# Third layer's probabilities turned by VectorE and DMA, the context one step later, and the context's split moved in the second feed-forward

## The chip, the cores and the metric

The kernel runs on one core of a Trainium2 chip. The metric is the time of one execution in device microseconds. Three runs of the kernel before gave 2253.87, 2254.23 and 2256.28 us; their median is 2254.23 us.

## What is computed

Four transformer layers run one after the other on x (16 batches of 128 tokens, 256 wide) and a context of the same shape. The change touches the third layer (called l2 in the code) and the feed-forward of the second (l1). The third layer has two cross-attentions in a row, with 16 heads of width 128, over 16 batches (cut from the reference):

```
qh = (q_in @ wq + bq)   kh = (kv_in @ wk + bk)   vh = (kv_in @ wv + bv)
kh, vh = each with one more key/value row (bias_k, bias_v)
logits = einsum('bqhk,bthk->bhqt', qh, kh) / sqrt(128)
weights = softmax(logits)
ctx = einsum('bhqt,bthk->bqhk', weights, vh);  x = x + ctx @ wo + bo
```

The kernel computes this per head and per group of four batches: 2 attentions x 16 heads x 4 groups = 128 steps. The einsum with vh sums over the 128 keys, so TensorE needs the probabilities with the keys on the partitions, while softmax leaves them with the queries on the partitions. Somewhere between the two they have to be turned.

## The kernel before

`attention2` is one block in which every engine runs its own part of one written list, `order2()`. The loop variable p is the place in the list and `step(stage, behind)` puts the stage of step s = p - behind there. Each engine executes in this order only the stages that it has a function for, so the list is the program of all five engines. What follows are the names that matter here.

At place p TensorE (PE) multiplies the queries (`query`, bank q_psum), then half of the output projection of an older step (`out_a`, o_psum), the keys (`key`, k_psum), the other half (`out_b`), then `turn` (L766: four 128x128 transposes of probs into t_psum, one instruction per batch), `score` (L756), half of a value projection (`value_a`), `context` (L776, probabilities times values into c_psum) and `value_b`. Products in full precision are three matmuls of high and low parts (L114 and L790). `turn` belongs to step p-1, `context` to p-1, and `out_a`/`out_b` to p-2.

VectorE (DVE) at place p makes the low part of the context (L910), the share of each probability (L933, L935), adds the value bias (`values_kept`, L920), adds the two output halves to x (L929), copies t_psum into PT (L901) and takes the maximum of the scores (L905). ScalarE (ACT) makes Q, K, the exponents into the one buffer probs (L833) and the high part of the context (L828). GpSimd (POOL) splits the weights of the heads ahead of their use (L664, L667). SyncE (SP) only issues DMAs: heads, value weights and value rows.

After 128 steps the pipeline drains over a few more places, and a block ends when all five engines have arrived.

The feed-forward of the second layer is the block before. Its list, `FEED_ORDER`, has four groups of eight `up` products and four `down` products. At its end GpSimd runs `split_context` (L2861, L2864): it splits the raw context, 2 x 2048 columns per partition, into the high and low parts that the third layer's keys and values need.

Of the kernel before, what the change touches and what calls it, by code (L numbers as in the profile page):

```python
# [426 lines left out]
STEPS2 = 2 * H * 4  # L427
HEAD_SLOTS = 6
# [13 lines left out]
def order2():  # L442
# [10 lines left out]
    def values(i):  # L453
        return [("value_a", 0, i), ("value_b", 0, i), ("values_kept", 0, i)]

    steps = [("stats", 0), ("value_weights", 0), ("scaled", 0), ("heads", 0), *values(0), ("stats", 1),
             ("normed", 0, 0), *values(1), ("normed", 0, 1), ("key", 0), ("heads", 1), *values(2), ("query", 0),
             ("biased", 0), ("heads", 2), ("heads", 3)]
    for p in range(STEPS2 + 6):
# [17 lines left out]
        step("out_b", 2)  # L477
        step("turn", 1)
# [5 lines left out]
        step("context", 1)  # L484
# [9 lines left out]
def attention2(c):  # L494
# [12 lines left out]
    with ExitStack() as ctx:  # L507
# [29 lines left out]
        PT = sb("PT", [P, BANK])  # L537
# [28 lines left out]
        t_full, t_free = sem("t_full"), sem("t_free")  # L566
        c_full, c_high, c_free = sem("c_full"), sem("c_high"), sem("c_free")
# [36 lines left out]
        def _(sync):  # L604
# [22 lines left out]
            def heads(j):  # L627
# [4 lines left out]
            def value_weights(n):  # L632
# [3 lines left out]
                if 2 <= n + 1 < 8:  # L636
                    sync.wait_ge(v_free, value_at["value_b", 4 * (n - 1) + 3, 3] + 1)
                    load_rows(n + 1)

            order.run({"heads": heads, "value_weights": value_weights})  # L640
# [69 lines left out]
        def _(pe):  # L710
# [58 lines left out]
            def values_summed(s):  # L769
                u, hh = s // 4, s % 4  # L770
                pe.wait_ge(t_free, turn_at["turn", s] + 1)
# [3 lines left out]
                for i in range(4):  # L775
                    last = pe.matmul(c_bank[:, i * S:(i + 1) * S], V[:, u % 2, i, hh * P:(hh + 1) * P],  # L776
                                     PT[:, i * S:(i + 1) * S], start=True, stop=True)
                last.then_inc(c_full, 1)

            def out(s, half):  # L780
# [3 lines left out]
                if n:  # L784
                    pe.wait_ge(o_free, n)
                for i in out_halves(s, half):
                    for m, (left, right) in enumerate(((0, 0), (0, 1), (1, 0))):
                        if left:
                            pe.wait_ge(c_free, s + 1)
                        last = pe.matmul(o_bank[:, i % 2 * D:(i % 2 + 1) * D], context[left][:, i * S:(i + 1) * S],  # L790
                                         wo[right], start=(m == 0), stop=(m == 2))
# [16 lines left out]
        def _(act):  # L808
# [28 lines left out]
            def probs_a(s):  # L837
                act.wait_ge(max_done, s + 1)
                if s:
                    act.wait_ge(t_full, turn_at["turn", s - 1] + 1)  # L840
# [32 lines left out]
        def _(dve):  # L873
# [23 lines left out]
            def turn(s):  # L897
                dve.wait_ge(t_full, turn_at["turn", s] + 1)
                if s:
                    dve.wait_ge(c_full, s)  # L900
# [2128 lines left out]
```

## Time and profile before

| | us |
|---|---|
| median of three runs | 2254.23 |
| the profiled execution, its own time | 2256.25 |
| its span (first to last instruction) | 2254.1 |
| the third layer's attention, from first SP issue to the block's end | 700.2 to 1739.4 |
| TensorE busy over the span | 2136.9 (95%) |
| VectorE busy | 1452.7 (64%) |
| ScalarE busy | 1279.3 (57%) |
| GpSimd busy | 651.8 (29%) |

The profile is one execution, so the sum of a prediction is made against 2256.25 us, and the median lies 2.0 us lower. TensorE's matmuls are pipelined: each row shows a duration that contains latency, and neighbouring rows overlap. What one costs the pace of a full TensorE is the distance between starts, not the duration.

### The profile page before, as it was taken

Reading aid. Unit: us, or ns where it says so; the run is one execution under the profiler, and the core shown is the slowest. Engines: PE = TensorE matmul, PEld = TensorE weight load, DVE = VectorE, ACT = ScalarE, POOL = GpSimd, SP = SyncE. Lnnn points to the kernel's source line nnn. Section 1 sums busy time; section 2 is a strip of 40 time slices with the busy share of each in tenths; the row PEclk is TensorE's granted clock in tenths of the full one; section 3 lists DMA queues with packets and bytes.
Section 4 is the critical chain, followed back from the end, with each engine's and each line's share of the span. In section 5 each row is a group of like instructions: output and inputs, shape, how many; then the busy total and the mean of one; then the engine's idle time right before and its main releaser. Section 6 shows DMA issues by size and latency. Waiting matters only on the chain. (4 is left out here: it accounts for less than half of the span.)

```text
span 2254.1 us, 47742 instructions
## 1 busy us (share of the span) xinstructions
PE 2136.9 (95%) x18208; PEld 1784.1 (79%) x18208; DVE 1452.7 (64%) x2828; ACT 1279.3 (57%) x3300; POOL 651.8 (29%) x661
## 2 busy tenths in 40 slices
PE   6999979999896999999999999999998999999899
PEld 4666656888685888888888888888887886776688
DVE  5788844555444756666666766666666449999963
ACT  3777754566543554444445544444455448988853
POOL 4444321111116422020303312030101127677711
PEclk9999999999998999999999999999998999999999
DMA  4000010000102000010100000000002120000000
GB/s 131 21 16 11 2 54 5 2 2 2 39 1 80 24 24 24 10 38 1 48 1 24 24 24 24 10 29 1 1 1 74 39 58 1 2 2 2 2 10 29
DMA packets 33661, 50.58 MB, mean 22 GB/s; under 512 B 2592, under 2 KB 22048, under 8 KB 32416
## 3 DMA queue, kind: packets, MB, share of 16 engines
q1 hardware_dynamic: 33440, 47.53, 6.9%
q8 instruction: 151, 2.47, 0.5%
q14 instruction: 70, 0.57, 0.1%
HBM read 45.43 MB, written 2.10 MB: 21 GB/s over the span
## 5 line engine op out<-in xcount | busy, mean ns | idle before, releaser
L833 ACT ACTIVATE l_probs<-l_s_psum,l_neg_max 128x129 f32<-128x129 f32 x512 | 183.1, 365 | 267.4 <-DVE l_neg_max L905 267.4
L929 DVE TENSOR_TENSOR x<-x,l_o_psum 128x512 f32<-128x512 f32 x256 | 174.9, 683 | 182.3 <-PE l_o_psum L790 182.3
L910 DVE SCALAR_TENSOR_TENSOR l_context_low<-l_c_psum,cols,l_context_high 128x512 fp32r<-128x512 f32 x128 | 95.8, 749 | 177.4 <-ACT l_context_high L828 177.2
L1461 DVE TENSOR_REDUCE l_neg_max<-l_psum 128x2 f32<-128x512 f32 x256 | 163.5, 683 | 50.2 <-PE l_psum L1251 49.8
L664 POOL TENSOR_TENSOR l_head_w_high<-l_head_raw,one 128x768 fp32r<-128x768 f32 x30 | 44.5, 1483 | 502.6 <-PE l_o_psum L790 502.6
L2513 POOL TENSOR_TENSOR l_probs<-l_probs,l_mask_add 128x512 f32<-128x512 f32 x128 | 161.7, 1284 | 76.9 <-DVE l_probs L2741 76.9
L821 ACT ACTIVATE l_KT<-l_k_psum,cols 128x512 f32<-128x512 f32 x128 | 88.1, 688 | 167.4 <-PE l_k_psum L114 167.4
L1390 ACT ACTIVATE l_PT<-l_psum 128x512 f32<-128x512 f32 x256 | 132.2, 602 | 56.9 <-PE l_psum L1279 56.9
L2683 ACT ACTIVATE l_probs<-l_probs,l_neg_max 128x128 f32<-128x128 f32 x512 | 159.7, 395 | 5.5 <-DVE l_neg_max L2748 5.1
L790 PE MATMUL l_o_psum<-l_head_w_high,l_context_high 128*128 128x256 f32 x512 | 144.7, 283 | 2.5 <-DVE x L929 1.7
L790 PE MATMUL l_o_psum<-l_head_w_high,l_context_low 128*128 128x256 f32 x512 | 144.2, 282 | 2.0 <-DVE l_context_low L910 2.0
L776 PEld LDWEIGHTS l_c_psum<-l_PT,values 128*128 128x128 f32 x1024 | 134.7, 192 | 12.5 <-DVE l_PT L901 1.9
L790 PE MATMUL l_o_psum<-l_head_w_low,l_context_high 128*128 128x256 f32 x512 | 143.5, 280 | 0.0
L114 PE MATMUL l_v_psum<-l_value_w_high,ctx_high 128*128 128x512 f32 x256 | 123.0, 480 | 15.2 <-DVE l_value_w_low L950 14.8
L776 PE MATMUL l_c_psum<-l_PT,values 128*128 128x128 f32 x1024 | 136.1, 276 | 0.9 <-DVE l_PT L901 0.8
L756 PE MATMUL l_s_psum<-l_KT,l_QT 128*128 128x129 f32 x1024 | 135.6, 274 | 0.8 <-ACT l_QT L815 0.8
L815 ACT ACTIVATE l_QT<-l_q_psum,l_query_bias 128x512 f32<-128x512 f32 x128 | 88.5, 691 | 76.0 <-PE l_q_psum L114 76.0
L756 PEld LDWEIGHTS l_s_psum<-l_KT,l_QT 128*128 128x128 f32 x1024 | 124.5, 191 | 1.2 <-ACT l_QT L815 1.2
L2132 DVE TENSOR_TENSOR l_mlp_h_low<-l_mlp_h,l_mlp_h_high 128x512 fp32r<-128x512 f32 x96 | 71.5, 747 | 72.6 <-ACT l_mlp_h L2046 71.9
L114 PE MATMUL l_mlp_psum<-l_mlp_w_high,l_mlp_h_high 128*128 128x256 f32 x384 | 111.0, 289 | 6.5 <-DVE l_mlp_h_low L2132 6.5
L2043 ACT ACTIVATE l_mlp_h_high<-l_mlp_psum,cols 128x512 fp32r<-128x512 f32 x96 | 66.2, 690 | 88.0 <-PE l_mlp_psum L114 80.5
L114 PE MATMUL l_mlp_psum<-l_mlp_w_high,l_mlp_h_low 128*128 128x256 f32 x384 | 109.6, 286 | 0.0
(320 smaller groups left out, 6343.0 us busy)
## 6 DMA issues: line engine op xcount, KB each, us to landing
l_head_raw<-in_l_heads SPq DMA_DIRECT2D x32, 384.0 KB, 3.0
l_w<-in_l_w SPq DMA_DIRECT2D x4, 1024.0 KB, 9.6
l_ctx_in<-in_ctx_T SPq DMA_DIRECT2D x16, 256.0 KB, 5.5
l_value_raw<-in_l_values SPq DMA_DIRECT2D x8, 512.0 KB, 3.7
l_value_rows<-in_l_rows SPq DMA_DIRECT2D x8, 512.0 KB, 4.9
l_x_in<-in_x_T SPq DMA_DIRECT2D x16, 128.0 KB, 2.2
l_x_in<-in_ctx_T SPq DMA_DIRECT2D x16, 128.0 KB, 2.7
values<-in_l_w SPq DMA_DIRECT2D x2, 1024.0 KB, 6.2
```

What stands on the lines that cost most here:

```text
L114: last = pe.matmul(out, left[a], right[b], start=(start and n == 0), stop=(stop and n == 2))
L756: last = pe.matmul(scores[:, i // 2, i % 2, :], QT[:, i * S:(i + 1) * S], KT[:, i, :], start=True, stop=True)
L776: last = pe.matmul(c_bank[:, i * S:(i + 1) * S], V[:, u % 2, i, hh * P:(hh + 1) * P], PT[:, i * S:(i + 1) * S], start=True, stop=True)
L790: last = pe.matmul(o_bank[:, i % 2 * D:(i % 2 + 1) * D], context[left][:, i * S:(i + 1) * S], wo[right], start=(m == 0), stop=(m == 2))
L815: act.activation(QT[:, :], q_bank[:, :], ACT.Identity, bias=query_bias[:, layer(s), head(s):head(s) + 1], scale=scale).then_inc(q_free, 1)
L833: last = act.activation(probs[:, i, :], scores[:, i // 2, i % 2, :], ACT.Exp, bias=neg_max[:, i:i + 1], scale=1.0, accum_out=den[:, i:i + 1])
L910: dve.scalar_tensor_tensor(out=context[1][:, :], in0=c_bank[:, :], scalar=vector("bias_v", s), in1=context[0][:, :].bitcast(F32), op0=ALU. ...
L929: dve.tensor_tensor(out=x, in0=x, in1=o_bank[:, :], op=ALU.add).then_inc(o_free, 1)
L1390: act.activation(PT[:, 2 * w + t, g, :], score_banks[g][:, :], ACT.Exp).then_inc(exp_done, 1)
L1461: dve.tensor_reduce(neg_max[:, u % 2, qt, at:at + 2], bank[:, :].rearrange("p (e k) -> p e k", e=2), AX, ALU.max, negate=True).then_inc(fr ...
L2513: pool.tensor_tensor(out=probs[:, s % SCORES3, :, :], in0=probs[:, s % SCORES3, :, :], in1=four(mask_add[:, mask_slot(u), :]), op=ALU.add) ...
L2683: last = act.activation(p, p, ACT.Exp, bias=neg_max[:, s % SCORES3, m:m + 1], scale=1.0)
```

## The change

Five things change.

1. For steps 0 to 126 TensorE's `turn` and VectorE's copy go. VectorE turns each 32x32 block of probs within its place (L943, one STREAM_TRANSPOSE of 128x512 into `turned`, two buffers). SyncE then moves the blocks: one DMA of the 256 KB tile to a DRAM tensor `moving`, a wait for its landing, and four DMAs of 64 KB back into PT, which now has two buffers. Together the transposed blocks and their moved places make the full transposes. Step 127 is turned on TensorE as before.
2. `context`, `context_low`, `out_a` and `out_b` run one place later (2, 3, 3 and 3 behind instead of 1, 2, 2, 2).
3. In an output half the two low-part matmuls come after all four high-part ones, so the wait for the low part (c_free) stands after four matmuls instead of two.
4. SyncE's loads get their own places in the list (`heads_next`, `values_next`, `rows_next`), between the `moved` stages.
5. In the second layer's feed-forward ScalarE rounds the context (four pieces of 1024 columns, after groups 0 and 1) and GpSimd subtracts (after the x bias of groups 1 and 2); `split_context` goes.

The core of the diff:

```diff
         steps.extend(("value_weights", n) for n in range(8) if values_at[n] == p)
         if p:
             step("query", 0)
-        step("context_low", 2)
+        step("context_low", 3)
         steps.extend([("normed", 10, 0)] if p == STEPS2 else [])
         step("share", 1)
+        step("out_a", 3)
+        step("moved", 1)
+        steps.extend(("heads_next", j) for j in range(2 * H) if heads_at[j] == p)
+        steps.extend(("values_next", n) for n in range(8) if values_at[n] == p)
+        steps.extend(("rows_next", n) for n in range(2, 8) if 16 * n - 18 == p)
         if 0 < p and p + 2 < STEPS2:
             steps.append(("values_kept", (p + 2) // 4, (p + 2) % 4))
-        step("out_a", 2)
...
-        step("out_b", 2)
-        step("turn", 1)
+        step("out_b", 3)
+        steps.extend([("turn", LAST2)] if p == STEPS2 else [])
         step("score", 0)
...
-        step("context", 1)
+        step("context", 2)
...
+            def moved(s):
+                if s == LAST2:
+                    return
+                i, before = s % 2, 16 * (s // 2)
+                sync.wait_ge(blocks_turned, s + 1)
+                if s >= 2:
+                    sync.wait_ge(landed[i], READS2 * before)
+                sync.dma_start(moving[i].rearrange("a j b x -> (a j) b x"),
+                               turned[:, i, :, :, :].rearrange("p b i x -> p b (i x)")).then_inc(sent[i], 16)
+                sync.wait_ge(sent[i], before + 16)
+                if s >= 2:
+                    sync.wait_ge(c_full, s - 1)
+                for a in range(4):
+                    sync.dma_start(PT[:, i, a, :, :].rearrange("p i x -> p (i x)"), moving[i, a].rearrange("j b x -> b j x"))\
+                        .then_inc(landed[i], 16)
...
             def values_summed(s):
                 u, hh = s // 4, s % 4
-                pe.wait_ge(t_free, turn_at["turn", s] + 1)
+                if s == LAST2:
+                    pe.wait_ge(t_free, turn_at["turn", s] + 1)
+                else:
+                    pe.wait_ge(landed[s % 2], 16 * READS2 * (s // 2 + 1))
...
+            def blocks(s):
+                if s == LAST2:
+                    return
+                i = s % 2
+                dve.wait_ge(probs_ready, s + 1)
+                if s >= 2:
+                    dve.wait_ge(sent[i], 16 * (s // 2))
+                dve.transpose(turned[:, i, :, :, :].rearrange("p b i x -> p i b x"),
+                              probs[:, :, 0:S].rearrange("p i (b x) -> p i b x", b=4)).then_inc(blocks_turned, 1)
...
+CONTEXT_HIGH = {0: (0, 1), 1: (2, 3)}
+CONTEXT_LOW = {1: (0, 1), 2: (2, 3)}
...
+    FEED_ORDER += [("ctx_low", _n) for _n in CONTEXT_LOW.get(_g, ())]
...
+    FEED_ORDER += [("ctx_high", _n) for _n in CONTEXT_HIGH.get(_g, ())]
```

The list decides where things stand. VectorE in the middle of the stage, one place p, before:

```order
L910 SCALAR_TENSOR_TENSOR l_context_low<-l_c_psum,cols,l_context_high 128x512
L933 RECIPROCAL l_rden<-l_den 128x4
L935 TENSOR_TENSOR l_probs<-l_probs,l_rden 128x4x128
L920 TENSOR_TENSOR values<-l_v_psum,l_value_rows 128x512
L929 TENSOR_TENSOR x<-x,l_o_psum 128x512 x2
L901 COPY l_PT<-l_t_psum 128x512
L905 TENSOR_REDUCE l_neg_max<-l_s_psum 128x4
```

The same place of the changed kernel:

```order
L976 RECIPROCAL l_rden<-l_den 128x4
L978 TENSOR_TENSOR l_probs<-l_probs,l_rden 128x4x128
L972 TENSOR_TENSOR x<-x,l_o_psum 128x512
L943 STREAM_TRANSPOSE l_turned<-l_probs 128x4x4x32
L963 TENSOR_TENSOR values<-l_v_psum,l_value_rows 128x512
L972 TENSOR_TENSOR x<-x,l_o_psum 128x512
L948 TENSOR_REDUCE l_neg_max<-l_s_psum 128x4
```

The first addition to x and the block transposes now stand ahead of the value bias (`values`), and the copy ahead of the maximum is gone.

TensorE where the stage drains, the last rows of `attention2` from the turn of step 127 on, before (the six output matmuls of step 127 follow twice):

```order
L766 MATMUL l_t_psum<-ident,l_probs 128x128 x4
L776 MATMUL l_c_psum<-l_PT,values 128x128 x4
L790 MATMUL l_o_psum<-l_head_w_high,l_context_high 128x256
L790 MATMUL l_o_psum<-l_head_w_low,l_context_high 128x256
L790 MATMUL l_o_psum<-l_head_w_high,l_context_low 128x256
```

And in the changed kernel, down to the context of step 127, after which the output of step 127 follows as above:

```order
L793 MATMUL l_t_psum<-ident,l_probs 128x128 x4
L806 MATMUL l_c_psum<-l_PT,values 128x128 x4
L819 MATMUL l_o_psum<-l_head_w_high,l_context_high 128x256
L819 MATMUL l_o_psum<-l_head_w_low,l_context_high 128x256
L819 MATMUL l_o_psum<-l_head_w_high,l_context_high 128x256
L819 MATMUL l_o_psum<-l_head_w_low,l_context_high 128x256
L823 MATMUL l_o_psum<-l_head_w_high,l_context_low 128x256 x2
L819 MATMUL l_o_psum<-l_head_w_high,l_context_high 128x256
L819 MATMUL l_o_psum<-l_head_w_low,l_context_high 128x256
L819 MATMUL l_o_psum<-l_head_w_high,l_context_high 128x256
L819 MATMUL l_o_psum<-l_head_w_low,l_context_high 128x256
L823 MATMUL l_o_psum<-l_head_w_high,l_context_low 128x256 x2
```

One whole round more (context, output a, output b, here of step 126) stands between the turn of step 127 and its context.

SyncE, two steps of the changed kernel with a head's load between them, where before only the loads stood:

```order
L658 DMA l_moving<-l_turned 128x512 [waits l2_landed1,l2_blocks_turned]
L664 DMA l_PT<-l_moving 128x1x128 [waits l0_rn_done,l2_sent1]
L664 DMA l_PT<-l_moving 128x1x128 x3
L616 DMA l_head_raw<-in_l_heads 128x768 [waits l2_heads_ready]
L658 DMA l_moving<-l_turned 128x512 [waits l2_landed0,l2_blocks_turned]
```

The load of a head now waits in the same queue as the moves, and a move behind it waits for GpSimd's `heads_ready`. (The name l0_rn_done is that of the semaphore which serves as c_full here.)

## Rows read from the trace of the kernel before

**Rows 1.** The page, busy time of TensorE, and its granted clock by slice.
```profile
PE 2136.9 (95%) x18208; PEld 1784.1 (79%) x18208; DVE 1452.7 (64%) x2828; ACT 1279.3 (57%) x3300; POOL 651.8 (29%) x661
...
PEclk9999999999998999999999999999998999999999
```
**Rows 2.** Stretches: length, busy PE, PEld, DVE, ACT, POOL, clock, DMA share, GB/s.
```profile
735.00:1719.00 984.00, 981.10 (x6287) 879.21 (x6286) 625.44 (x1100) 478.67 (x1533) 182.52 (x119) 1.00 0.06 18
1719.00:1740.00 21.00, 14.25 (x78) 11.71 (x76) 10.11 (x18) 6.63 (x16) 2.68 (x3) 0.75 0.26 97
```
**Rows 3.** Timeline, TensorE, one step: start, duration, engine, line, what.
```profile
1202.98 0.40 PE L114 MATMUL l_q_psum<-n_high,l_head_w_high 128*128 128x512 f32 x1
...
1204.35 0.28 PE L790 MATMUL l_o_psum<-l_head_w_high,l_context_high 128*128 128x256 f32 x1
...
1205.06 0.39 PE L114 MATMUL l_k_psum<-ctx_high,l_head_w_high 128*128 128x512 f32 x1
...
1207.17 0.60 PE L766 MATMUL l_t_psum<-ident,l_probs 128*128 128x128 f32 x4
1207.61 1.06 PE L756 MATMUL l_s_psum<-l_KT,l_QT 128*128 128x129 f32 x8
1208.42 0.48 PE L114 MATMUL l_v_psum<-l_value_w_high,ctx_high 128*128 128x512 f32 x1
...
1209.21 1.05 PE L776 MATMUL l_c_psum<-l_PT,values 128*128 128x128 f32 x8
```
**Rows 4.** Timeline, VectorE, the same step and the maximum before it.
```profile
1200.89 0.70 DVE L905 TENSOR_REDUCE l_neg_max<-l_s_psum 128x4 f32<-128x516 f32 x1
...
1205.32 0.68 DVE L929 TENSOR_TENSOR x<-x,l_o_psum 128x512 f32<-128x512 f32 x1
...
1208.70 0.70 DVE L905 TENSOR_REDUCE l_neg_max<-l_s_psum 128x4 f32<-128x516 f32 x1
```
**Rows 5.** VectorE's groups, 740 to 1700 us: busy us, mean ns, idle before.
```profile
L901 DVE COPY l_PT<-l_t_psum 128x512 f32<-128x512 f32 x122 | 83.4, 684 | 0.0
```
**Rows 6.** Timeline, second feed-forward: ScalarE's idle, and the end of the block.
```profile
624.65 0.69 ACT L2043 ACTIVATE l_mlp_h_high<-l_mlp_psum,cols 128x512 fp32r<-128x512 f32 x1 [12.01 <-PE l_mlp_psum L114]
...
691.66 0.42 DVE L2140 TENSOR_TENSOR x<-x,l_mlp_psum 128x256 f32<-128x256 f32 x1 [2.46 <-PE l_mlp_psum L114]
...
695.41 4.50 POOL L2864 TENSOR_TENSOR ctx_low<-ctx_raw,ctx_high 128x2048 fp32r<-128x2048 f32 x1
...
700.24 1.41 DVE L879 BATCH_NORM_STATS2 l_stats<-x 128x6 f32<-128x256 f32 x4 [8.16 <-PEq L2258]
```
**Rows 7.** Timeline, the drain of the third layer's attention.
```profile
1729.53 1.03 PE L766 MATMUL l_t_psum<-ident,l_probs 128*128 128x128 f32 x4 [0.93 <-ACT l_n_full L855]
1731.35 2.08 PE L776 MATMUL l_c_psum<-l_PT,values 128*128 128x128 f32 x8 [0.78 <-DVE l_PT L901]
...
1738.29 0.41 PE L790 MATMUL l_o_psum<-l_head_w_high,l_context_low 128*128 128x256 f32 x1
...
1738.74 0.69 DVE L929 TENSOR_TENSOR x<-x,l_o_psum 128x512 f32<-128x512 f32 x1 [1.81 <-PE l_o_psum L790]
```
**Rows 8.** DMA issues: count, KB each, us to landing; and SyncE's timeline.
```profile
l_head_raw<-in_l_heads SPq DMA_DIRECT2D x32, 384.0 KB, 3.0
l_x_in<-in_x_T SPq DMA_DIRECT2D x16, 128.0 KB, 2.2
l_wq<-in_l_wq SPq DMA_DIRECT2D x1, 64.0 KB, 2.5
...
4.67 0.43 SPq L93 DMA_DIRECT2D l_wk<-in_l_wk  x1
5.14 0.43 SPq L93 DMA_DIRECT2D l_wv<-in_l_wv  x1
```
**Rows 9.** Timeline, GpSimd, the last head split ahead of the steps.
```profile
725.97 1.82 POOL L667 TENSOR_TENSOR l_head_w_low<-l_head_raw,l_head_w_high 128x768 fp32r<-128x768 f32 x1
```
**Rows 10.** The page's costliest group: busy us, mean ns, idle before and releaser.
```profile
L833 ACT ACTIVATE l_probs<-l_s_psum,l_neg_max 128x129 f32<-128x129 f32 x512 | 183.1, 365 | 267.4 <-DVE l_neg_max L905 267.4
```

More of the change, by code:

```diff
@@ L785, in out @@
                     pe.wait_ge(o_free, n)
+                first = 2 * half
                 for i in out_halves(s, half):
[L787 to L791, printed above, removed]
+                    for right in range(2):
+                        pe.matmul(o_bank[:, i % 2 * D:(i % 2 + 1) * D], context[0][:, i * S:(i + 1) * S], wo[right],
+                                  start=(i == first and right == 0), stop=False)
+                pe.wait_ge(c_free, s + 1)
+                for i in out_halves(s, half):
+                    last = pe.matmul(o_bank[:, i % 2 * D:(i % 2 + 1) * D], context[1][:, i * S:(i + 1) * S], wo[0],
+                                     start=False, stop=(i != first))
                 last.then_inc(o_full, 1)
@@ L953, in _ @@
             order.run({"heads": heads, "value_weights": value_weights,
-                       "stats": stats_of, "scaled": scaled, "turn": turn, "score": maxima,
+                       "stats": stats_of, "scaled": scaled, "turn": turn, "moved": blocks, "score": maxima,
                        "context_low": context_low, "values_kept": values_kept, "out_a": lambda s: add(s, 0),
@@ L2021, in quarter2, with context_piece, ctx_high @@
         return [w[:, 2 * q:2 * q + 2, :] for w in (self.w2[:, :, :], self.w2_high[:, :, :], self.w2_low[:, :, :])]
+    def context_piece(self, n):
+        at = slice(n % 2 * 8, n % 2 * 8 + 8)
+        return [part[:, n // 2, at, :] for part in [self.c.ctx_raw] + self.c.ctx_parts]
     def scalar(self, act):
+        def ctx_high(n):
+            if self.context:
+                raw, high, _ = self.context_piece(n)
+                if n == 0:
+                    act.wait_ge(self.c.ctx_loaded, 32)
+                act.activation(high, raw, ACT.Copy).then_inc(self.c.ctx_high, 1)
         def w1_high(q):
@@ L2246, with feed_forward @@
         FEED_ORDER += [("stored", 4 * _g + _n)]
-def feed_forward(c, name, func, finish, load_ahead=None, parts=None, beside=None, late=None, early=None):
+def feed_forward(c, name, func, finish, load_ahead=None, parts=None, context=False, late=None, early=None):
     nc = c.nc
@@ L2266, in sem @@
             return sems[-1]
-        feed = Feed(c, sb, sem, name, func, finish, parts, late, early)
+        feed = Feed(c, sb, sem, name, func, finish, parts, late, early, context)
         banks = [ctx.enter_context(nc.psum_tensor(f"{name}_mlp_psum{i}", [P, BANK], F32)) for i in range(8)]
@@ L2855, in load_context @@
                 sync.dma_start(c.ctx_raw[:, t, :, :], tile).then_inc(c.ctx_loaded, 16)
-        def split_context(pool):
-            pool.wait_ge(c.ctx_loaded, 32)
-            for t in range(2):
-                raw, high, low = (part[:, t, :, :] for part in [c.ctx_raw] + c.ctx_parts)
-                pool.tensor_tensor(out=high, in0=raw, in1=c.one[:, :].unsqueeze(2).to_broadcast([P, B, S]), op=ALU.mult)\
-                    .then_inc(c.ctx_high, 1)
-                pool.wait_ge(c.ctx_high, t + 1)
-                pool.tensor_tensor(out=low, in0=raw, in1=high.bitcast(F32), op=ALU.subtract)
         def tokens_T(scope, name, side="left"):
```

51 lines of the change are left out of this document (30 added, 21 removed).

## The prediction

> **What bounds the kernel now.** I read the page first: TensorE is busy 95% of the span, and its clock is at full speed but for two slices [rows 1]. Then the stretches, since the share is a mean over stages. In the third layer's steady part, 735 to 1719 us, TensorE is busy for 981.1 of 984.0 us at the full clock (the 2.4 GHz level), VectorE for 64% of it, DMA for 6% [rows 2]. So in this stage time is TensorE's work, and what another engine does counts only if it makes TensorE wait. Third, the timeline of one step. Two maxima of VectorE start 7.81 us apart [rows 4], and that is the step; the turn's four transposes start at 1207.17 and the scores behind them at 1207.61 [rows 3]. The row says 0.60 us, but the next work starts after 0.44: the pace counts, 0.44 us. Fourth, the two seams. The second feed-forward's last addition ends at 692.08, and VectorE starts in the next block at 700.24; in between only GpSimd works, its last split ends at 699.91 [rows 6]. At the other end, from 1719 on, TensorE is busy for 14.25 of 21 us at a mean clock of 0.75: a drain, bound by a chain of waits [rows 2, 7].
>
> **The turn leaves TensorE.** 127 steps x 0.44 = 55.9 us. A few of these lie in the drain, where TensorE waits anyway, so I take 55.3. The step becomes 7.81 - 0.44 = 7.37 us.
>
> **VectorE.** Its copy (684 ns) goes and one instruction that turns the blocks of the same 128x512 comes. No row shows one. From below it is bounded by nothing less than half a copy, 0.34 us (more would need two elements a cycle, and no 512-column row of this stage is under 0.68), from above by twice a copy, 1.37. I take the value nearest to the copy's row, 0.69 [rows 5]. What matters is its place: it stands ahead of `values_kept`, which frees the bank for `value_a`. Counted from the step's start (queries, 1202.98): the first addition to x runs from 2.34 to 3.02 [rows 3, 4], the blocks then to 3.71, the value bias (0.68) to 4.39. TensorE wants the bank at 1208.42 - 1202.98 - 0.44 = 5.00. Slack 0.6 us, so it costs nothing; the point from which it does is a duration of about 1.15 us (with 0.15 for signals, an estimate). The maximum starts when the scores are done, as before; the copy ahead of it is gone.
>
> Rule against it: the Trainium skill, "VectorE: DVE Perf Modes", section "The three transpose paths", gives 311 ns for one 128x128 bf16 tile on VectorE. If this scaled by tile, four would take 1.24 us, an estimate. No run here shows it yet. It would put the sum 0.1 us per step, some 11 us, above mine.
>
> **The round trip.** TensorE's `context` no longer waits for a copy but for the landing of four reads. Its length: a load of 128 KB lands after 2.2 us and one of 384 KB after 3.0, so the 256 KB to DRAM take 2.6 by the mean of the two; then SyncE's wait ends (0.1, estimate); four issues at a distance of 0.47 put the last 1.4 us behind the first, and a load of 64 KB lands after 2.5 [rows 8]. Sum 6.6 us. Bounds: 5.5 (2.0 and 2.0 for the two hops, both a bit under the fastest row) and 9.6 (a 384 KB head load of 3.0 us wholly in front). What it may take: the blocks end 3.71 us into a step, the context of the same step stands two places on, 1209.21 - 1202.98 - 0.44 = 5.79 into the next step. 7.37 + 5.79 - 3.71 = 9.45 us. So 2.8 us are spare, and the wait ends before TensorE comes. With a stall x each step, the step gets longer and the context moves back in it, so the time allowed grows by 2x: a trip of L costs (L - 9.45)/2 per step.
>
> SyncE's queue is the other thing passed: heads_next stands behind `moved` and waits for GpSimd's split of that head (some 3.3 us, its second half 1.82 [rows 9]). GpSimd starts it when the output of three steps ago is done, 4.2 us into the step before [rows 3], so ends about 0.2 into this one; SyncE comes there when its reads are issued, 3.7 + 0.1 + 2.6 + 1.9 = 8.3, or 0.9 into it. No wait, cost nothing; without that cover up to 3 us on some 26 steps, of which 2.8 are spare.
>
> Rule against it: the Trainium skill, "DMA: Bandwidth & Descriptors", section "Latency and other measured facts", puts an access of HBM at 0.2 us on average and 2 us at high load. The stage's DMA share is 6% [rows 2], so I take the first. With 1.8 us more on both hops the trip would be 10.2 us, which costs 0.4 per step, and the time would be near 2244; it is one of the ways into the rival below.
>
> **The start.** Context and output of step 0 come a place later, which takes 0.8 (as the scores, 1207.61 to 1208.42) + 1.4 (twice 1204.35 to 1205.06) = 2.2 us of TensorE's work out of the first places [rows 3] (it comes back in the drain). Against it: `moved(0)` stands behind heads_next(3), which waits for GpSimd's split that ends at 727.79 [rows 9]; plus 0.4 for the load's issue and 6.6 for the trip is 734.8, and TensorE would come for the context at about 733 (estimate: place 2 less two turns, a context and an output). A stall of about 1.3 to 1.8 us, at most 4.8 with the head's load in front. Net -0.6.
>
> **The drain.** One round more stands between the turn of step 127 and its context. The round of step 127 in the trace: context from 1731.35, output ended at 1738.70, block end 1739.43 [rows 7]. Now the context of step 126 starts right behind the turn, at 1730.56, since it waits for no copy; its round takes 7.35, then the last round its 8.08 to the block's end: 1745.99, against 1739.43, +6.6. In each of both rounds the low-part matmuls wait behind four others instead of two (0.4 to 0.5 us less at this clock): -0.9. Sum +5.7. It runs at the lower level (1.2 GHz) as the round of before did: eight context matmuls took 2.08 us there and 1.05 in the steady part.
>
> **The feed-forward.** ScalarE gets four roundings of 1024 columns, about 1.1 us each (estimate, 512 columns take 0.69), two after each of groups 0 and 1. It sat idle for 12.0 us there, waiting for TensorE's down products [rows 6]: hidden, and if it weren't, 4.4 us. GpSimd's subtractions, 9 us in all (half of the tensor took 4.50), lie in groups 1 and 2, long before the end. At the end nothing is left after the last addition at 692.08; the attention's own seam took 0.3 us (last split 699.91, first work 700.24), so the next block starts at 692.4 instead of 700.2: -7.8.
>
> **Sum.** -55.3 - 0.6 + 5.7 - 7.8 = -58.0 us. 2256.25 - 58.0 = 2198.2 for an execution like the profiled one; the median of the runs lies 2.0 lower, so 2196.
>
> **The rivals.**
> A. VectorE is late: the blocks take 1.15 to 1.6 us, `values_kept` frees the bank late and TensorE waits at `value_a`. For: no row has this instruction, and it reads and writes in short runs of 32. Against: the 512-column rows of VectorE beside it lie between 0.68 and 0.70 [rows 4, 5]. At 1.37 us it is 0.22 per step, 28 us: 2224.
> B. SyncE's queue: a move waits behind a head whose split GpSimd has late. At 1 us net on 26 steps, 26 us: 2222. For: both are in one queue. Against: the slack above.
> C. The other side: the round trip binds every step. It decides in favour of the kernel before from 58/127 = 0.46 us stall per step, or L = 10.4 us. For: two dependent hops have no row here, a store to DRAM that is read at once neither. Against: the rows give 6.6, and even a head's load in front leaves 9.6. At L = 11.5 the stall is 1.0 per step, 130 us: 2326. From 9.45 to 10.4 it is a part of the gain that is lost, 2196 to 2254.
> D. The gain is not there because something else of the step is as long as TensorE's work. The chain runs from scores to maximum to exponents to the next scores: the maximum starts 0.28 after the scores and takes 0.70 [rows 3, 4], four exponents of 0.37 [rows 10] and the reads of their sums some 2.3; 3.3 of 7.37, and ScalarE's largest idle time is its wait for the maximum, so no. If it were so, only the seams, the start and the drain would count (-2.7), and the time would be 2252.
>
> **Chances.** Forecast (2188 to 2203) 0.68. A 0.10, B 0.08, C between 9.45 and 10.4 0.05, C beyond 0.07, others (D, or a drain much shorter) 0.02. The range: 2187 to 2225 takes in the forecast's own and A and B; what is outside is mostly C. Less than 0.2% (4.5 us) cannot be told from no change here; only a narrow part of C and A falls there, 0.02. Faster 0.91, slower 0.07.
>
> **What would show it.** Right: TensorE's transposes of probs only once, four matmuls; steps 7.37 us apart; `context` rows with no wait on PT after the first; a group of 127 block transposes near 0.69; the third layer's first instruction at 692.4; the block's end about 6 us later behind the last scores than before. Wrong: a wait of the context matmuls for a DMA in each step (C, and its size gives L), of the value matmuls for VectorE (A), waits that recur only after head loads (B), or ScalarE's roundings delaying TensorE in the feed-forward.

## The result, and the profile after

The changed kernel takes 2240.2 us (median of four runs, 2235.11 to 2241.93), the kernel before took 2254.05 us beside it (2253.46 to 2256.28). The ratio is 0.9932, with a 95% interval of 0.9916 to 0.9949. It is faster by 14 us (0.7%, with an interval that stays below 1), but 58 us were forecast: 2240 lies outside the range of 2187 to 2225. The profiled execution took 2238.5 us, with a span of 2236.5, 17.6 less than before.

Where the 17.6 went, from VectorE's rows in both timelines. The first line ends with its seventh subtraction for the low part of h in the feed-forward's first group (611.31 before, 607.27 now), the second with its first work in the third layer:

| stretch | before | after | difference | forecast |
|---|---|---|---|---|
| up to the seventh `up` product of the second feed-forward's first group | 611.3 | 607.3 | -4.0 | 0 |
| from there to the third layer's first work | 88.9 | 81.1 | -7.8 | -7.8 |
| first work to the fourth maximum | 43.5 | 46.2 | +2.7 | -0.6 |
| fourth to last maximum (124 steps) | 978.9 | 966.8 | -12.1 | -54.6 |
| last maximum to the block's end | 16.8 | 21.7 | +4.9 | +5.7 |
| the rest | 514.7 | 513.5 | -1.2 | 0 |

The first and the last row lie ahead of and behind all code that the change touches, and I don't count them as a gain. Most of the first is spread between executions: the changed kernel and the eleven kernels below have the same code up to this place, and their profiles reach it between 607.2 and 610.8 us, the changed kernel's at 607.3. So the 14 us between the medians are the better measure of the gain. One row of the table holds nearly the whole error, 42.5 us: 124 steps that should have lost 0.44 us each lost 0.10.

The page of the changed kernel, the lines that answer to [rows 1]:

```profile
PE 2106.0 (94%) x17700; PEld 1734.0 (78%) x17700; DVE 1473.7 (66%) x2828; ACT 1282.1 (57%) x3304; POOL 646.0 (29%) x661
...
PEclk8999999999999999999999999999998999999999
```

The stretches, as in [rows 2], the steady part and the drain:

```profile
735.00:1690.00 955.00, 938.21 (x5689) 817.89 (x5688) 624.16 (x1074) 467.70 (x1502) 176.42 (x114) 1.00 0.27 85
1705.00:1724.00 19.00, 12.13 (x54) 10.57 (x54) 6.40 (x11) 4.30 (x8) 2.56 (x2) 0.59 0.32 117
```

TensorE was busy for all but 2.9 of 984 us in this stage before; now it is idle for 16.8 of 955. The granted clock is unchanged at 1.00. The waits of TensorE's weight loads, 728 to 1705 us (total us, times, longest):

```profile
PEld l_s_psum L783 <- issue: 36.0, 122, 0.3
...
PEld l_c_psum L806 <- DMA l_PT<-l_moving: 0.9, 1, 0.9
```

The context's wait for the trip through DRAM, which I had feared, came once in this stretch (and once in the start, below). What came in every step is 0.30 us at the scores, a line that the profile before doesn't have. "Issue" means that no releaser was found, so the timeline has to name it. One step of the changed kernel, all engines (columns as in [rows 3]):

```profile
1340.74 0.21 ACT L866 ACTIVATION_READ_ACCUMULATOR l_probs<-l_s_psum,l_neg_max 128x1 f32 x1
...
1343.33 0.40 PE L114 MATMUL l_k_psum<-ctx_low,l_head_w_high 128*128 128x512 f32 x1
...
1343.56 0.28 PE L819 MATMUL l_o_psum<-l_head_w_high,l_context_high 128*128 128x256 f32 x1
...
1343.76 0.69 ACT L854 ACTIVATE l_KT<-l_k_psum,cols 128x512 f32<-128x512 f32 x1 [1.32 <-PE l_k_psum L114]
...
1344.03 0.40 PE L823 MATMUL l_o_psum<-l_head_w_high,l_context_low 128*128 128x256 f32 x2
...
1344.52 0.97 PEld L783 LDWEIGHTS l_s_psum<-l_KT,l_QT 128*128 128x128 f32 x8 [0.30 <-issue]
1344.55 1.13 PE L783 MATMUL l_s_psum<-l_KT,l_QT 128*128 128x129 f32 x8
```

The same place before, the last key matmul and ScalarE's copy:

```profile
1206.22 0.41 PE L114 MATMUL l_k_psum<-ctx_low,l_head_w_high 128*128 128x512 f32 x1
...
1206.66 0.69 ACT L821 ACTIVATE l_KT<-l_k_psum,cols 128x512 f32<-128x512 f32 x1 [1.33 <-PE l_k_psum L114]
```

The scores read KT, ScalarE's copy of the keys. From the start of the last key matmul to the end of this copy pass 1.12 us now (1343.33 to 1344.45) and passed 1.13 before (1206.22 to 1207.35), so the copy is as fast as it was. Before, TensorE had the output half and the turn to do meanwhile, and began the scores at 1207.61 [rows 3], 0.26 after the copy's end. Now only the output half is left, which takes 0.71 us and would let the scores start at 1344.27 (1343.56 + 0.71), 0.18 before the copy is done. They start 0.10 behind it. So 0.44 us of work went, some 0.3 of waiting came, and the scores, which took 0.81 us to the next work before, take 0.88 now.

What the moves cost by themselves, a group of VectorE (740 to 1690 us, as in [rows 5]) and two DMA issues (as in [rows 8]):

```profile
L943 DVE STREAM_TRANSPOSE l_turned<-l_probs 128x512 f32<-128x512 f32 x122 | 85.9, 704 | 0.0
```
```profile
l_moving<-l_turned SPq DMA_DIRECT2D x127, 256.0 KB, 2.0
...
l_head_raw<-in_l_heads SPq DMA_DIRECT2D x32, 384.0 KB, 4.4
```

The block transposes take 0.70 us. The Trainium skill, "VectorE: DVE Perf Modes", section "The three transpose paths", gives 311 ns per 128x128 bf16 tile; scaled by tile to 1.24 us, an estimate that I had weighed, it doesn't hold for these four fp32 tiles in one instruction, and the measurement decides.

The two seams. The feed-forward's last addition and the third layer's first work, as in [rows 6], and ScalarE's and GpSimd's part:

```profile
608.48 2.01 ACT L2076 ACTIVATE ctx_high<-ctx_raw 128x1024 fp32r<-128x1024 f32 x2
...
634.05 5.39 POOL L2155 TENSOR_TENSOR ctx_low<-ctx_raw,ctx_high 128x1024 fp32r<-128x1024 f32 x2
...
687.62 0.42 DVE L2200 TENSOR_TENSOR x<-x,l_mlp_psum 128x256 f32<-128x256 f32 x1 [2.45 <-PE l_mlp_psum L114]
688.36 1.40 DVE L912 BATCH_NORM_STATS2 l_stats<-x 128x6 f32<-128x256 f32 x4 [0.32 <-PEq L2322]
```

The drain, TensorE and the last addition to x, as in [rows 7]:

```profile
1708.16 0.84 PE L793 MATMUL l_t_psum<-ident,l_probs 128*128 128x128 f32 x4 [0.93 <-ACT l_n_full L888]
1708.79 1.92 PE L806 MATMUL l_c_psum<-l_PT,values 128*128 128x128 f32 x8
...
1715.43 1.91 PE L806 MATMUL l_c_psum<-l_PT,values 128*128 128x128 f32 x8
...
1722.29 0.69 DVE L972 TENSOR_TENSOR x<-x,l_o_psum 128x512 f32<-128x512 f32 x1 [1.80 <-PE l_o_psum L823]
```

### The profile page after: what moved, and what is told of

Same layout as the page of the kernel before. It is cut to its first block and busy times, and to the rows that moved or that the text cites. A ratio compares the mean times of both kernels' runs of the same rounds, so it can differ in the third digit from the quotient of the medians.

```text
span 2236.5 us, 47492 instructions
## 1 busy us (share of the span) xinstructions
PE 2106.0 (94%) x17700; PEld 1734.0 (78%) x17700; DVE 1473.7 (66%) x2828; ACT 1282.1 (57%) x3304; POOL 646.0 (29%) x661
## 5 line engine op out<-in xcount | busy, mean ns | idle before, releaser
L783 PE MATMUL l_s_psum<-l_KT,l_QT 128*128 128x129 f32 x1024 | 144.6, 283 | 17.1 <-issue 1.6
L948 DVE TENSOR_REDUCE l_neg_max<-l_s_psum 128x4 f32<-128x516 f32 x128 | 89.0, 696 | 76.9 <-PE l_s_psum L783 76.9
L819 PE MATMUL l_o_psum<-l_head_w_high,l_context_high 128*128 128x256 f32 x512 | 134.7, 285 | 3.8 <-DVE x L972 2.2
L819 PE MATMUL l_o_psum<-l_head_w_low,l_context_high 128*128 128x256 f32 x512 | 133.1, 282 | 0.0
L819 PEld LDWEIGHTS l_o_psum<-l_head_w_high,l_context_high 128*128 128x128 f32 x512 | 97.1, 190 | 17.3 <-issue 4.2
```

What stands on the lines that cost most here:

```text
L783: last = pe.matmul(scores[:, i // 2, i % 2, :], QT[:, i * S:(i + 1) * S], KT[:, i, :], start=True, stop=True)
L819: pe.matmul(o_bank[:, i % 2 * D:(i % 2 + 1) * D], context[0][:, i * S:(i + 1) * S], wo[right], start=(i == first and right == 0), stop=False)
L948: dve.tensor_reduce(neg_max[:, :].rearrange("p (j i) -> p j i", j=2), scores, AX, ALU.max, negate=True)\
```

## The experiments

Theory 1: the step is held by the keys' copy, and TensorE's removed work was its cover. Rival 2: the DMA traffic of the moves (share 0.27, before 0.06) slows TensorE. Later ones concern the start and the trip. Each experiment is an edit of the changed kernel unless it says otherwise; ratios are to the kernel before on the same chip. A third explanation, called rival 3 in some expectations, is that the scores wait for the exponents of the step before, whose bank they overwrite. The timeline above speaks against it: the last row of the exponents ends at 1340.95, 3.6 us ahead of the scores.

**e3_filler.** Unneeded work in front of the scores:

```diff
                 pe.wait_ge(q_free, s + 1)
+                for i in range(4):
+                    pe.transpose(q_bank[:, i * S:(i + 1) * S], c.ident[:, :], c.ident[:, :])
                 pe.wait_ge(k_free, s + 1)
```

> Edit: four transposes of the identity into the bank of the queries, whose content ScalarE has already taken, stand between the outputs and the scores in each of the 128 steps; they compute nothing that is used. They take 0.44 us of TensorE each step. Theory 1: they fill the wait for the keys' copy, so the step rises by no more than 0.44 - 0.37 = 0.07 us, to 7.82, and the time by 9 us to about 2249. Rival 2 (TensorE's work itself is slower): 0.44 us more per step, 8.18, about 2296 us. Rival 3: as theory 1.

Measured 2248.5 us, ratio 0.9978 [0.9969, 0.9987]. The step is 7.82 and the wait at the scores gone; TensorE, 745 to 1690 us:

```profile
745.00:1690.00 945.00, 942.60 (x6036) 845.57 (x6036) 608.37 (x1046) 456.66 (x1468) 170.78 (x109) 1.00 0.26 85
```

0.44 us of added work cost 0.09 per step, with the same DMA share. Rival 2 falls: with the traffic still there, TensorE does the work of the kernel before in the time of the kernel before (7.82). Theory 1 passes its sharpest test.

**e1_context_first.** Real work as the cover, the context:

```diff
         steps.extend([("turn", LAST2)] if p == STEPS2 else [])
+        step("context", 2)
         step("score", 0)
...
         step("probs_a", 0)
-        step("context", 2)
```

> Edit: the context product of the step two back stands ahead of the scores instead of behind them. Theory 1 (the turn had covered the wait for ScalarE's copy of the keys, and only 0.71 us of output matmuls are left between the last key matmul and the scores): 0.8 us of work now covers that wait of 0.36 us, the step goes from 7.74 to 7.37 us, and the time from 2240 to about 2194 us, unless the reads back into PT land too late for a context that comes 0.8 us earlier in the step; then waits of the context for a DMA appear and a part is lost. Rival 2 (DMA traffic or the strided PT makes TensorE's own work slower): nothing changes, step 7.74, 2240 us. Rival 3 (the scores wait for the exponents of the step before): the context ahead covers as well, but then ScalarE's exponents end just before the scores, and the step stays above 7.6.

Measured 2226.8 us, ratio 0.9871 [0.9854, 0.9888]. The commonest step is the 7.37 of the theory, but the time lies 33 us above the 2194 expected for it: the context now stands 1.6 us earlier, and often meets its reads. The mean of the 124 steps is 7.70. The waits that name the reads hold only a part of the excess; how the rest follows from them was not worked out. Waits, and one of them in the timeline:

```profile
PE l_c_psum L806 <- DMA l_PT<-l_moving: 15.4, 19, 3.7
```
```profile
1327.13 0.47 SPq L626 DMA_DIRECT2D l_value_rows<-in_l_rows  x1
1327.95 0.70 DVE L943 STREAM_TRANSPOSE l_turned<-l_probs 128x512 f32<-128x512 f32 x1
1328.68 0.33 SPq L658 DMA_DIRECT2D l_moving<-l_turned  x1
...
1332.80 2.21 SPq L664 DMA_DIRECT2D l_PT<-l_moving  x4
...
1338.34 0.94 PE L806 MATMUL l_c_psum<-l_PT,values 128*128 128x128 f32 x6 [0.34 <-DMA l_PT<-l_moving]
```

From the blocks' end (1328.65) to the landing (1338.34) it is 9.7 us: here the write stands behind a 512 KB load, and the reads start 4.1 us after it instead of 2.0. For undisturbed steps of the changed kernel I estimate 7.6 from the packets in the trace, of which the last mostly end 7.0 to 7.8 us behind the blocks.

**e2_value_first.** The same with the first value half as the cover, and its bias (`values_kept`) ahead of the first addition:

```diff
+        if 0 < p and p + 2 < STEPS2:
+            steps.append(("values_kept", (p + 2) // 4, (p + 2) % 4))
         step("out_a", 3)
...
-        if 0 < p and p + 2 < STEPS2:
-            steps.append(("values_kept", (p + 2) // 4, (p + 2) % 4))
...
+        if p + 3 < STEPS2:
+            steps.append(("value_a", (p + 3) // 4, (p + 3) % 4))
         step("score", 0)
...
-        if p + 3 < STEPS2:
-            steps.append(("value_a", (p + 3) // 4, (p + 3) % 4))
```

> Edit: the first half of the value projection stands ahead of the scores, and VectorE's value bias ahead of its first addition to x (as in the kernel before). The landing in PT keeps its time. Theory 1: step 7.37 to 7.45 us (some of the cover may be lost where the bank of the values comes free late, or where the exponents, which now start 0.7 us later in the step, delay the share and the additions), 2194 to 2204 us. Rival 2: 7.74, 2240 us. Rival 3: the scores come later in the step and so do the exponents, no gain: 7.74 or more.

Measured 2232.9 us, ratio 0.9917 [0.9905, 0.993], steps of 7.66: the expected 7.37 to 7.45 and 2194 to 2204 us were missed. The wait left the scores and moved one stage up, to the second output half, which needs the first addition to x, and that addition now stands behind the value bias on VectorE:

```profile
PEld l_o_psum L819 <- issue: 57.9, 106, 1.7
```

**e5_turn_kept.** The turn back on TensorE and the copy on VectorE, no moves through DRAM; the later places, the order in the output halves and the feed-forward stay as changed:

```diff
-        step("moved", 1)
...
-        steps.extend([("turn", LAST2)] if p == STEPS2 else [])
+        step("turn", 1)
...
```

> Edit: no block transposes and no moves; TensorE turns every step as in the kernel before and VectorE copies, but context and output stay one place later and the rest of the change stays. It tells what the later place costs alone. Theory 1: the step is 7.82 us again with no wait at the scores; start -2 us, drain +5, seam -8: about 2249 to 2251 us. Rival 2: as theory 1 here, but without the moves TensorE's work must get faster by 0.3 us per step other than the turn, i.e. each group of matmuls has a smaller distance than in the changed kernel.

Measured 2243.0 us, ratio 0.9948 [0.9935, 0.9962], steps of 7.82 and no wait at the scores. So neither the later places nor the new order in the output halves makes the wait. The time is 6 us below the expected 2249 to 2251; why is open. **e4_seam** is the kernel before with only the feed-forward's part.

> The kernel before with the feed-forward's part of the change alone: the context's split by ScalarE and GpSimd inside the second feed-forward; attention is as before. Theory 1 (the keys' copy limits the step, so the moves bring little and the seam brings the rest): the third layer starts 7.8 us earlier, steps stay 7.82, about 2246. Rival (the seam is hidden elsewhere and the gain of the change comes from the attention's part): no change, 2253 to 2255.

Measured 2243.8 us, ratio 0.9956 [0.994, 0.9973], steps of 7.82, about as expected. VectorE at the seam waits 0.32 us instead of 8.16 [rows 6]:

```profile
689.21 1.41 DVE L879 BATCH_NORM_STATS2 l_stats<-x 128x6 f32<-128x256 f32 x4 [0.32 <-PEq L2279]
```

The two agree with each other within their intervals. They lie about 3 us above the changed kernel, but its interval overlaps with both, so this rest isn't clear of noise: most of the change's gain is the seam, and the turn through DRAM brought a few us at most. The profiles show what cancels: from the fourth to the last maximum the changed kernel takes 966.8 us and e5 975.9, but from the first to the fourth it takes 26.8 and e5 22.7.

**e6_first_move.** The start. In the changed kernel SyncE waits for GpSimd's split of a head before its first write, and TensorE then waits for the reads:

```profile
705.84 9.77 SPq L616 DMA_DIRECT2D l_head_raw<-in_l_heads  x3
715.65 0.43 SPq L658 DMA_DIRECT2D l_moving<-l_turned  x1
719.42 2.39 SPq L664 DMA_DIRECT2D l_PT<-l_moving  x4
...
725.16 1.88 PE L806 MATMUL l_c_psum<-l_PT,values 128*128 128x128 f32 x8 [2.28 <-DMA l_PT<-l_moving]
```

The edit puts that head's load behind the first write:

```diff
-             ("biased", 0), ("heads", 2), ("heads", 3), *(("heads_next", j) for j in range(1, 4))]
+             ("biased", 0), ("heads", 2), ("heads", 3), *(("heads_next", j) for j in range(1, 3))]
...
         step("moved", 1)
+        steps.extend([("heads_next", 3)] if p == 1 else [])
```

> The changed kernel with one entry moved: on SyncE the load behind head 3 stands behind the first write to DRAM, not ahead of it. Theory on the start (the first write waited for GpSimd's split of head 3, and its transfer ran behind that head's load): the first context waits under 0.5 us instead of 2.28, the first steps are 2 to 4 us shorter in sum, and the time is 2236 to 2238. Rival (the start is set by the one place more and by VectorE's chain, not by the queue): no change, 2240.

Measured 2233.4 us, ratio 0.9907 [0.9892, 0.9922]. The wait is gone, and the third distance between maxima is 8.18 instead of 12.33 us; the 124 steps behind it differ little (965.1 and 966.8 us). The 6.8 us between the medians, which come from two chips, are more than the 2 to 4 expected, and the time is below the expected 2236 to 2238.

**e7_keys_in_halves** and **e8_halves_and_first_move.** ScalarE copies the keys in two halves, and the products of two batches wait for the first half only (TensorE's waits change with it, not shown); e8 has the edit of e6 too.

```diff
-                act.activation(KT[:, :, 0:S], k_bank[:, :].rearrange("p (i k) -> p i k", i=4), ACT.Identity,
-                               bias=vector("bk", s), scale=1.0).then_inc(k_free, 1)
+                for n in range(2):
+                    act.activation(KT[:, 2 * n:2 * n + 2, 0:S],
+                                   k_bank[:, 2 * n * S:(2 * n + 2) * S].rearrange("p (i k) -> p i k", i=2), ACT.Identity,
+                                   bias=vector("bk", s), scale=1.0).then_inc(k_free, 1)
```

> The changed kernel with ScalarE's copy of the keys in two halves of two batches each, so that the first two score matmuls wait for a copy of 256 columns only. ScalarE has one instruction more per step (about 0.2 us), the context keeps its place, which leaves the trip's allowance near 9.5 us. Theory 1: the wait at the scores goes or falls under 0.05, the step is 7.37 to 7.42, 127 steps bring 41 to 46 us: 2194 to 2200. Rival 2 (TensorE's pace or the trip through DRAM limits the step): 7.7 as now, 2238 or more. Third: the first half is early enough but the second or the exponents come late on ScalarE: 7.45 to 7.6, about 2210 to 2225.

> Both edits together: keys copied in halves, and the load behind head 3 after the first write to DRAM. By theory 1 and the theory on the start the gains add: 2 to 4 us below the version with halves alone, 2190 to 2197. If the start's stall is only moved to the second head's load, the two are equal within 1 us.

Measured 2219.2 us, ratio 0.9846 [0.9832, 0.9861], and 2213.8 us, ratio 0.982 [0.9806, 0.9835]. The step is 7.57: the direction of theory 1, half of its size, and 7.57 and 2219.2 lie where the third alternative put them, though the reason is another. The two runs differ by 5.4 us, expected were 2 to 4. e7's scores, and the copies' group from 740 to 1675 us:

```profile
1341.01 0.84 ACT L856 ACTIVATE l_KT<-l_k_psum,cols 128x256 f32<-128x256 f32 x2 [1.32 <-PE l_k_psum L114]
...
1341.28 0.40 PE L824 MATMUL l_o_psum<-l_head_w_high,l_context_low 128*128 128x256 f32 x2
...
1341.63 1.13 PE L784 MATMUL l_s_psum<-l_KT,l_QT 128*128 128x129 f32 x8
1342.52 0.48 PE L114 MATMUL l_v_psum<-l_value_w_high,ctx_high 128*128 128x512 f32 x1
```
```profile
L856 ACT ACTIVATE l_KT<-l_k_psum,cols 128x256 f32<-128x256 f32 x244 | 102.4, 472 | 162.1 <-PE l_k_psum L114 162.1
```

One copy of half the columns lasts 0.47 us, not 0.35 (the two overlap, 0.84 together), so the first half is ready at about 1341.48. The output ends its pace at 1341.51, the scores start at 1341.63 (0.12 late) and take 0.89 to the next work instead of 0.81. With the 0.20 of both, 7.57 is explained: the copy is still what ends last.

**e9_longer_trip.** The tile is written to DRAM twice, one after the other, before it is read:

```diff
-                sync.wait_ge(sent[i], before + 16)
+                sync.wait_ge(sent[i], 2 * before + 16)
+                sync.dma_start(moving[i].rearrange("a j b x -> (a j) b x"),
+                               turned[:, i, :, :, :].rearrange("p b i x -> p b (i x)")).then_inc(sent[i], 16)
+                sync.wait_ge(sent[i], 2 * before + 32)
...
```

> The changed kernel, but SyncE writes the turned tile to DRAM twice, the second time after the first has landed, and reads only then: the trip is 2.0 to 2.1 us longer in each of 127 steps. By the trace of the changed kernel the trip takes about 7.6 us and may take about 10.2 there (7.74 + 5.79 + 0.37 - 3.67), so 9.7 is still hidden in most steps, and only steps with a head's load in front stall: 2240 to 2255. If the trip were already at the end of its allowance (the rival that the trip binds), the step grows by about 1 us: over 2300.

Measured 2409.2 us, ratio 1.0692 [1.0677, 1.0707]: 169 us above the changed kernel, 1.33 per step. My expectation failed and the rival's number, over 2300, stood. SyncE's waits, whole run, then its timeline:

```profile
SPq L661 <- DMA l_moving<-l_turned: 472.3, 127, 6.8
```
```profile
1388.23 2.20 SPq L667 DMA_DIRECT2D l_PT<-l_moving  x4
1390.91 0.32 SPq L658 DMA_DIRECT2D l_moving<-l_turned  x1
1394.62 0.33 SPq L661 DMA_DIRECT2D l_moving<-l_turned  x1
1396.63 2.20 SPq L667 DMA_DIRECT2D l_PT<-l_moving  x4
```

SyncE's waits in the changed kernel, 728 to 1705 us:

```profile
SPq L658 <- DVE l_turned L943: 395.0, 123, 4.8
SPq L664 <- DMA l_moving<-l_turned: 217.0, 125, 3.7
```

I had counted the trip as a latency: 2 us more, 2.5 spare. But SyncE does every hop itself and waits in between, so its round is a resource. In the changed kernel it stands idle 3.2 us per step (395.0 / 123) for VectorE. The second write takes 2.0 of these; and the first, now issued 0.5 us behind the last read (1390.43 to 1390.91), is waited for 3.7 us (472.3 / 127) instead of 1.74 (217.0 / 125). The two together are 4.0 us, more than the 3.2 that were free, and the head loads come on top. From 745 to 1690 us SyncE now waits for VectorE in only 49 of 103 steps, and TensorE for the reads in 90. That the reads in front of it delay the write was not tried apart, but e9's own trace bears it out: first writes issued within 0.5 us of the last read's issue land after 4.0 us (median of 60), and those issued 1.5 us or more behind it after 2.0 (median of 11). Those between, of which many stand behind another load too, take 3.4 to 5.1. In the changed kernel nearly all writes stand 2 us or more behind the reads.

**e10_value_b_late** and **e11_context_then_value_a.** To cover the keys' copy with useful work and leave the context's place alone: the second value half goes ahead of the next scores (with the edit of e6, keys copied whole). Then in e11 the context moves ahead of the first value half.

```diff
-        if 0 < p and p + 2 < STEPS2:
-            steps.append(("values_kept", (p + 2) // 4, (p + 2) % 4))
...
         step("out_b", 3)
+        if 0 < p and p + 2 < STEPS2:
+            steps.append(("value_b", (p + 2) // 4, (p + 2) % 4))
+            steps.append(("values_kept", (p + 2) // 4, (p + 2) % 4))
         step("score", 0)
-        if p + 3 < STEPS2:
-            steps.append(("value_a", (p + 3) // 4, (p + 3) % 4))
         step("probs_a", 0)
         step("context", 2)
+        if p + 3 < STEPS2:
+            steps.append(("value_a", (p + 3) // 4, (p + 3) % 4))
         step("probs_b", 0)
-        if p + 3 < STEPS2:
-            steps.append(("value_b", (p + 3) // 4, (p + 3) % 4))
```

(This is e11, without the edit of e6; in e10 `value_a` keeps its place ahead of `probs_a`.)

> The changed kernel with the later load of head 3, the keys' copy whole, and one stage moved in the written order: the second half of the value matmuls (0.71 us) stands ahead of the scores of the next step, not at the step's end, and the value bias on VectorE between the second addition to x and the maximum. TensorE then has 0.71 + 0.71 us of work between the last key matmul and the scores, and the copy needs 1.1. Theory 1: the wait at the scores is gone, the step is 7.37 to 7.40, 127 steps bring 43 to 47 us against the version with only the later load (2233): 2187 to 2192. If VectorE's longer chain makes the first addition late for the second output (slack 0.1 us by the trace), the step is 7.4 to 7.6 with a wait at the output's matmuls: 2192 to 2215.

> The kernel before this one (second half of the values ahead of the scores) with the context ahead of the first half of the values, so the order is output, second value half, scores, context, first value half. There the step was 7.58 with the wait at the scores gone: the trace shows the first value matmul 0.26 us behind the last score instead of 0.11, since VectorE's value bias (after the second addition) frees the bank only then. With the context (0.81 us) in between, the bank is free in time. Expected: no wait at scores nor at the values, and one gap fewer between matmuls of 128 and of 512 columns (0.09): step 7.28 to 7.32, 127 x 0.28 = 36 us below 2220: 2182 to 2190. If instead something else of the step is 7.5 long, or the context now waits for its reads: 2200 to 2225, with a wait at the context's matmuls.

e10 measured 2220.1 us, ratio 0.9858 [0.9839, 0.9876], steps of 7.58, which misses the expected 2187 to 2192 and also the 2192 to 2215 of its alternative: there is no wait at the scores, but a new one at the first value half. Its timeline:

```profile
1343.17 0.69 DVE L972 TENSOR_TENSOR x<-x,l_o_psum 128x512 f32<-128x512 f32 x1 [0.65 <-PE l_o_psum L823]
...
1343.67 1.06 PE L783 MATMUL l_s_psum<-l_KT,l_QT 128*128 128x129 f32 x8
1343.87 0.69 DVE L963 TENSOR_TENSOR values<-l_v_psum,l_value_rows 128x512 f32<-128x512 f32 x1
...
1344.71 0.47 PE L114 MATMUL l_v_psum<-l_value_w_high,ctx_high 128*128 128x512 f32 x1
```

Scores of 0.81 us would leave TensorE at 1344.48, and of the 0.89 that e11 shows for them in this place at 1344.56. The value bank is free at 1344.56 too (1343.87 + 0.69), and its matmul starts 0.15 later, at 1344.71. e11 measured **2201.3 us** (2196.25 to 2202.7), ratio 0.9762 [0.9748, 0.9776], the fastest of all. The same place, and the steady part:

```profile
1342.05 1.05 PE L783 MATMUL l_s_psum<-l_KT,l_QT 128*128 128x129 f32 x8
1342.94 1.05 PE L806 MATMUL l_c_psum<-l_PT,values 128*128 128x128 f32 x8
1343.75 0.48 PE L114 MATMUL l_v_psum<-l_value_w_high,ctx_high 128*128 128x512 f32 x1
```
```profile
735.00:1675.00 940.00, 927.93 (x5790) 826.35 (x5789) 643.32 (x1105) 465.69 (x1533) 181.51 (x120) 1.00 0.27 88
```

Its commonest step is 7.37, and the mean of the 124 steps 7.52, against 7.89 in the kernel before. The expectation of 7.28 to 7.32 and 2182 to 2190 was missed: the scores take 0.89 to the context, not 0.81, and a few steps of 8 to 12 us, near the change of attention and in the start, still hold waits for the reads and for the low part.

## Why the prediction was wrong

1. **What bounds the kernel, and its clock**: right as a description. TensorE was full, and no idle time showed another limit. The error lies in what I made of that.
2. **"The turn leaves TensorE ... The step becomes 7.81 - 0.44 = 7.37"**: this step failed: the term of -55.3 us was worth -12.1 over the 124 steps of the table. A full engine tells nothing of what stands right behind its work. I priced each wait that the change adds, and none that the removed work had covered. The steady step became 7.73, with 0.30 us of waiting at the scores. Rival D had the right form, something else as long as TensorE's work, but I examined one chain in it (scores, maximum, exponents) and dropped D on that, to a share of 0.02 together with others. The short chain is the other input of the scores: key matmul, ScalarE's copy, scores. It was readable before: copy 1206.66 to 1207.35, scores at 1207.61, so 0.26 of slack less 0.10 for the signal, against 0.44 taken away (the 0.10 is that of the changed kernel's trace, 1344.45 to 1344.55; the rows before don't have it). That gives a step of 7.81 - 0.16 = 7.65 at best, and with the other terms of the sum a time of about 2231. Measured are 7.73; of the rest of 0.08, 0.07 is the slower scores (0.88 instead of 0.81). What shows the cause are e3 (work put back in front of the scores is nearly free), e7 (a shorter copy of the keys shortens the step) and e11 (other useful work as cover gives 7.37).
3. **VectorE**: right, 0.70 us for 0.69, and no wait for it at `value_a`.
4. **The round trip**: not on the path, as forecast, but longer (7.6 us against 6.6 undisturbed, 9.7 behind a load in e1). The write landed after 2.0 us and not 2.6, but the last packets of the reads end some 3.4 us (median) behind the last read's issue, where I had 2.5. And I took its length for a sum of hops that stay as they are. In e9 2.0 us were added to it, but from the blocks' end to the context 12.7 us passed (median), not some 9.7, since SyncE's round ran full and the hops got slower. Put into my form with the allowance of 10.2, (12.7 - 10.2)/2 = 1.25, this comes near the 1.33 measured; the length was wrong, not the halving.
5. **SyncE's queue and the start**: -0.6 forecast, +2.7 measured. I had put the stall at 1.3 to 1.8 us; it was 2.3 at the context, and the chain behind it was late as well. e6 shows that it was the order of one load: with it moved, the first to the fourth maximum take 22.6 us, against 26.8 in the changed kernel and 23.6 before.
6. **The drain**: right, +5.7 forecast, +4.9 measured. The mean granted clock of the stretch is 0.59; from 1712 us on it is 0.50, the lower level, as it was before from 1734 on.
7. **The feed-forward**: right, -7.8 forecast and measured, in e4 alone too (8.16 - 0.32). ScalarE's roundings (2.01 us for two) were hidden.

With 7.37 as e11's commonest step, the forecast's number for the step was attainable; it needed a cover for the keys' copy that the change didn't bring. That e11's time lies in the forecast's own range doesn't make the forecast right: it is another kernel, with further edits.

## What to carry to other kernels

Before work is taken from a full engine, list what its next instruction reads, and for each input how long it had been ready; the smallest of these slacks, less the time of the signal, is the most that can be gained, unless other work is moved into the place, as in e11. A step that TensorE fills for 99.7% can still have 0.16 us between its limit and the next one. And an engine that issues a dependent chain of DMAs and waits in between has a round of its own: count its free time per step beside the latency.

## What the runs showed of the hardware

- A write of 256 KB to DRAM lands after 2.0 us; four reads of 64 KB each take SyncE 2.2 us to issue, 0.55 apart, where plain loads went out 0.47 apart [rows 8].
- With these moves in the queue the heads' loads of 384 KB land after 4.4 us instead of 3.0 ([rows 8], and e5, which has no moves), and in e9 a write issued within 0.5 us of the reads lands after 4.0 us (median of 60).
- ScalarE's copy of 256 columns from PSUM takes 0.47 us, of 512 columns 0.69: halving it saves 0.22, not half (two halves in a row take 0.84).
- Eight score matmuls take 0.81 us behind the turn's short ones, and 0.88 to 0.89 right behind a wait (changed kernel, e7) or behind matmuls of 512 columns (e11).
